# Layer 0 of a two-layer decoder: the context's sixteen key/value products placed at other points of the rounds

## The reference, cut to what matters

```
x = layernorm(x + L0_linear_attention(x))         # 16 heads; q and k normalised per head, scores squared, causal
x = layernorm(x + L0_cross_attention(x, context)) # q, k rms-normed; softmax over the context's 64 tokens
x = layernorm(x + L0_experts(x))                  # 16 experts, top 4, and 2 shared
x = layernorm(x + L1_attention(x))
x = layernorm(x + L1_cross_attention(x, context)) # k = context @ Wk.T, v = context @ Wv.T, 32 heads
x = layernorm(x + L1_experts(x))                  # 8 experts, top 2
```

## Time and profile before

| | us |
|---|---|
| median of 3 runs | 1344.89 |
| lowest, highest | 1341.75, 1347.87 |
| the profiled execution | 1342.68 |
| its span in the profile | 1340.8 |
| TensorE busy in the span | 1170.7 |
| layer 0, up to the first product of the experts' stage | 375.0 |
| mean granted clock of TensorE | 0.932 |

### The profile page before, as it was taken

How to read it: one execution, slowest core, us unless ns; L and a number is a source line. 1 busy time by engine, 2 the same in 40 slices (tenths; PEclk the granted TensorE clock), 3 DMA queues, 4 the chain that set the end, 5 groups by cost and what they waited for, 6 DMA issues and landing times. The chain is left out here.

```text
span 1340.8 us, 29170 instructions
## 1 busy us (share of the span) xinstructions
PE 1170.7 (87%) x10358; PEld 908.3 (68%) x10359; DVE 482.8 (36%) x1215; ACT 531.6 (40%) x1320; POOL 427.2 (32%) x542
## 2 busy tenths in 40 slices
PE   5878988988899759999977888888965999999998
PEld 2576776766546437777755666666653989989997
DVE  1235364554375012323334555544249100000322
ACT  1314435334433213333444566665420434333342
POOL 2022020121036882777624443111104400020343
PEclk9879798899999999999997999998867999999999
DMA  4039619021271434565471110000006665555573
GB/s 148 17 113 363 223 54 334 1 57 59 77 275 70 141 135 121 150 188 149 125 281 66 33 33 17 18 17 2 1 4 211 213 202 162 169 185 185 177 245 103
DMA packets 115225, 171.87 MB, mean 128 GB/s; under 512 B 17424, under 2 KB 92800, under 8 KB 113664
## 3 DMA queue, kind: packets, MB, share of 16 engines
q1 hardware_dynamic: 88640, 127.15, 29.2%
q0 software_dynamic: 9696, 26.75, 6.1%
q10 hardware_dynamic: 16784, 16.49, 3.7%
HBM read 105.07 MB, written 65.27 MB: 127 GB/s over the span
## 5 line engine op out<-in xcount | busy, mean ns | idle before, releaser
L2440 PE MATMUL bank<-m_XGT,m_w 128*128 128x128 f32 x1248 | 150.0, 279 | 1.9 <-issue 1.9
L2440 PEld LDWEIGHTS bank<-m_XGT,m_w 128*128 128x128 f32 x1248 | 146.4, 196 | 3.0 <-issue 2.7
L2454 PE MATMUL bank<-w,m_HT 128*128 x624 | 141.0, 379 | 0.0
L2454 PEld LDWEIGHTS bank<-w,m_HT 128*128 128x128 f32 x624 | 115.7, 190 | 14.1
L2272 ACT ACTIVATE m_HT<-bank,m_b 128x128 f32<-128x128 f32 x312 | 89.1, 369 | 89.7 <-PE bank L2440 77.8
L1478 PE MATMUL bank<-m_W,m_XGT 128*128 x316 | 110.6, 473 | 10.9 <-ACT m_XGT L1337 8.3
L1103 POOL DMA_INDIRECT GA<-ys,r_pos x64 | 64.5, 1008 | 58.3 <-DVE m_US L1419 39.4
L1337 ACT ACTIVATE m_XGT<-bank 128x256 f32<-128x256 f32 x79 | 30.3, 384 | 130.5 <-DVE m_US L1419 84.4
L1478 PEld LDWEIGHTS bank<-m_W,m_XGT 128*128 128x128 f32 x316 | 54.9, 194 | 31.9 <-issue 15.2
L1411 DVE TENSOR_TENSOR m_H<-bank,m_SG 128x176 f32<-128x176 f32 x79 | 27.0, 341 | 136.2 <-ACT m_SG L1341 105.0
L2232 POOL DMA_INDIRECT m_GA<-ys,r_pos x32 | 31.3, 978 | 130.4 <-SPq L2187 121.4
(11 more groups left out here) (356 smaller groups left out, 2441.6 us busy)
## 6 DMA issues: line engine op xcount, KB each, us to landing
m_w<-in_m_w SPq DMA_DIRECT2D x35, 1024.0 KB, 5.3
xs<-zeros SPq DMA_DIRECT2D x1, 10112.0 KB, 34.2
ys<-zeros SPq DMA_DIRECT2D x1, 10112.0 KB, 33.9
ys<-m_US ACTq DMA_DIRECT2D x79, 128.0 KB
m_GS<-xs SPq DMA_DIRECT2D x72, 128.0 KB
w<-in_m_w SPq DMA_DIRECT2D x8, 1024.0 KB, 17.7
m_W<-in_w SPq DMA_DIRECT2D x2, 2816.0 KB, 12.7
xs<-zeros SPq DMA_DIRECT2D x1, 4992.0 KB, 19.8
```

Source lines behind the costliest of these rows:

```text
L2440: last = nc.tensor.matmul(BU[i][:, c * P:(c + 1) * P], w1[:, b, m, lo:lo + P], XGT[:, b % 2, m * P:(m + 1) * P], start=m == 0, stop=m == K ...
L2454: last = nc.tensor.matmul(BY[b % 2][:, 0:DIM], HT[:, b % 2, c, :], w2[:, bass.ds(e, 1), c, :], start=c == 0, stop=c == CH - 1)
```

## The change

Six of the sixteen kv products go to stage 2 of rounds 0, 2 and 4, where `la_var` lies: in each, one in front of the variances and one among them, after the second of the four tiles. In the prologue, whose variances have no kv product, the first `la_v` product of group 0 is placed among them instead. The other ten stand in rounds 6 and 7, in the counts (2, 1, 1, 1) each. Rounds 8 and 9 have none.

A product among the variances and the variances themselves are signalled together (`then_inc(pj.full, 2)`) after the last variance. On ScalarE the product in front is emptied before `exps` of 2 and 3, the one among after the copies of turned weights. The first six tiles are emptied into the last 512 columns of XTA, which the router fills in rounds 8 and 9, and not into `SQK`. Wkv and the first two context tiles are loaded at the start. SyncE's queue follows the order of `fill`: each store, load and zero fill is issued when the use that it depends on comes up in that order.

```diff
-    kv_tiles = iter(range(TILES))
-    for i, counts in ((PAIRS - 2, (1, 1, 1, 1)), (PAIRS - 1, (1, 2, 1, 1)), (PAIRS, (2, 1, 1, 1)), (PAIRS + 1, (2, 0, 0, 0))):
+    kv_tiles = iter(("kv", t, 0) for t in range(TILES))
+    among = {0: ("la_v", 0, 0)}
+    for g in range(1, GROUPS):
+        front, among[g] = next(kv_tiles), next(kv_tiles)
+        fill[2 * (g - 1), 2] = [front] + fill[2 * (g - 1), 2] + [among[g]]
+    KV_EARLY = 2 * (GROUPS - 1)
+    for i, counts in ((PAIRS - 2, (2, 1, 1, 1)), (PAIRS - 1, (2, 1, 1, 1)), (PAIRS, (0, 0, 0, 0))):
         for s, n in enumerate(counts):
-            fill[i, s] += [("kv", next(kv_tiles), 0) for _ in range(n)]
+            fill[i, s] += [next(kv_tiles) for _ in range(n)]
...
+        def kv_staged(t):
+            return (XTA[:, t % 2, TOKENS - GTOK:] if t < KV_EARLY else SQK[:, t % 2, :])
...
+                load_channels(0)
+                load_context(0)
                 sp.dma_start(kvw, io["xb_wkv"].rearrange("(m p) o -> p m o", p=P)).then_inc(fx.ld_kc[0], 16)
                 context(0)
                 context(1)
...
+                for name, g, n in [use for i in range(-1, ROUNDS) for s in range(4) for use in fill[i, s]]:
+                    use = name, g, n
+                    if name == "kv":
+                        pj.wait_emptied(sp, use)
+                        sp.dma_start(fx.kv[g * P:(g + 1) * P, :], kv_staged(g)).then_inc(fx.kv_kept[g % 2], 16)
+                        if g % 2 and g // 2 + 2 < PAIRS:
+                            context(g // 2 + 2)
+                    elif use == ("la_v", g, 1) and g + 1 < GROUPS:
+                        pj.wait_full(sp, use)
+                        load_channels(g + 1)
+                    elif use == ("xa_v", g, 1):
+                        pj.wait_full(sp, use)
+                        if g + 1 < GROUPS:
+                            load_context(g + 1)
+                            if g == 0:
+                                sp.wait_ge(fx.ready, fx.READY)
+                                zero(fx.xs, fx.slots_zeroed, fx.NS0)
+                            elif g == 1:
+                                zero(fx.ys, fx.slots_zeroed, fx.NS0)
+                            else:
+                                zero(fx.xs1, fx.slots_zeroed1, fx.NS1)
+                                zero(fx.ys1, fx.slots_zeroed1, fx.NS1)
+                        else:
+                            shared_weights()
...
-                def inputs(i, s):
+                def inputs(i, s, later=False):
                     for use in fill[i, s]:
                         name, g, m = use
+                        if (use in among.values()) != later:
+                            continue
                         if name == "kv":
                             pj.wait_full(act, use)
                             if g >= 2:
                                 act.wait_ge(fx.kv_kept[g % 2], 16 * (g // 2))
-                            else:
+                            if g == KV_EARLY:
                                 pj.wait_full(act, ("xa_ks", GROUPS - 1, 0))
-                            nc.scalar.activation(SQK[:, g % 2, :], pj.bank(use)[:], ACT.Copy).then_inc(pj.emptied["A"], 1)
+                            nc.scalar.activation(kv_staged(g), pj.bank(use)[:], ACT.Copy).then_inc(pj.emptied["A"], 1)
...
+                    inputs(i, 2, True)
...
+                def keys_and_values(use):
+                    t = use[1]
+                    pe.wait_ge(fx.ld_kc[t // 2 % 2], context_at(t // 2))
+                    return product(nc, pj.bank(use)[:], chunks(KC_T[:, t // 2 % 2], t % 2), [kvw[:, m, :] for m in range(KC)])
+                def values(use):
+                    _, g, n = use
+                    for t in range(2):
+                        last = product(nc, pj.bank(use)[:, t * DIM:(t + 1) * DIM], chunks(XTIN, 2 * n + t),
+                                       [wv[:, m, :] for m in range(KC)])
+                    return last
+                def variance_steps(g, step):
+                    pj.wait_emptied(pe, ("la_k", g, 1))
+                    pj.before_fill(pe, ("la_var", g, 0))
+                    for t in range(TG):
+                        step(t)
+                        last = variances(g, t)
+                        if t == 1:
+                            pj.before_fill(pe, among[g])
+                            (values if g == 0 else keys_and_values)(among[g])
+                    last.then_inc(pj.full, 2)
...
+                    def turn_weights(r):
+                        pe.wait_ge(xw_ready.sem, xw_ready.at(j, r))
+                        for c in range(4):
+                            last = nc.tensor.transpose(SB[r][:, c * P:(c + 1) * P], WX[:, r, c * P:(c + 1) * P],
+                                                       fx.ident[:])
+                        last.then_inc(pt_full.sem, 1)
+                    beside = xa(i) and any(u[0] == "la_var" for u in fill[i, 2])
                     if beside:
-                        pj.before_fill(pe, beside[0])
-                        pj.wait_emptied(pe, ("la_k", beside[0][1], 1))
+                        front, (_, g_next, _), _ = fill[i, 2]
+                        pj.before_fill(pe, front)
+                        keys_and_values(front).then_inc(pj.full, 1)
+                        variance_steps(g_next, turn_weights)
                     else:
                         inputs(i, 2)
-                    if xa(i):
-                        for r in range(RG):
-                            pe.wait_ge(xw_ready.sem, xw_ready.at(j, r))
-                            for c in range(4):
-                                last = nc.tensor.transpose(SB[r][:, c * P:(c + 1) * P], WX[:, r, c * P:(c + 1) * P],
-                                                           fx.ident[:])
-                            last.then_inc(pt_full.sem, 1)
-                            if beside:
-                                last = variances(beside[0][1], r)
-                    if beside:
-                        last.then_inc(pj.full, 1)
+                        if xa(i):
+                            for r in range(RG):
+                                turn_weights(r)
```

More of the change, by code:

```diff
@@ L292, in context, with shared_weights @@
                         "(m p) t -> p m t", p=P)).then_inc(fx.ld_kc[p % 2], 16)
[L294 to L302 removed]
+                def shared_weights():
+                    sp.wait_ge(fx.padded, 1)
+                    for m in range(KC):
+                        for i in range(2):
+                            sp.dma_start(fx.S13[:, m, i, 0:HS].rearrange("p (e h) -> p e h", e=SHARED),
+                                         io["w13"][m, :, E0:EALL, i * I0:(i + 1) * I0]).then_inc(fx.ld_sh, 16)
+                    for c, lo, n, e, at in ((0, 0, P, 0, 0), (1, 0, I0 - P, 0, P), (1, I0 - P, 2 * P - I0, 1, 0),
+                                            (2, 0, HS - 2 * P, 1, 2 * P - I0)):
+                        sp.dma_start(fx.S2[lo:lo + n, c, :], io["w2"][at:at + n, E0 + e, :]).then_inc(fx.ld_sh, 16)
+                load_channels(0)
+                load_context(0)
                 sp.dma_start(kvw, io["xb_wkv"].rearrange("(m p) o -> p m o", p=P)).then_inc(fx.ld_kc[0], 16)
@@ L315, in _ @@
-                for t in range(TILES):
-                    pj.wait_emptied(sp, ("kv", t, 0))
-                    sp.dma_start(fx.kv[t * P:(t + 1) * P, :], SQK[:, t % 2, :]).then_inc(fx.kv_kept[t % 2], 16)
-                    if t % 2 and t // 2 + 2 < PAIRS:
-                        context(t // 2 + 2)
+                for name, g, n in [use for i in range(-1, ROUNDS) for s in range(4) for use in fill[i, s]]:
[22 more added lines that the diff above has]
+                            shared_weights()
@@ L679, in inputs @@
                         name, g, n = use
+                        if use in among.values():
+                            continue
+                        if name == "la_var":
+                            variance_steps(g, lambda t: None)
+                            continue
                         pj.before_fill(pe, use)
@@ L682, in inputs @@
                         if name == "kv":
-                            pe.wait_ge(fx.ld_kc[g // 2 % 2], context_at(g // 2))
-                            last = product(nc, bank[:], chunks(KC_T[:, g // 2 % 2], g % 2), [kvw[:, m, :] for m in range(KC)])
+                            last = keys_and_values(use)
                         elif name in ("la_q", "la_k"):
@@ L690, in inputs @@
                                            [XTIN[:, m, :] for m in range(KC)])
-                        elif name == "la_var":
-                            pj.wait_emptied(pe, ("la_k", g, 1))
-                            for t in range(TG):
-                                last = variances(g, t)
                         elif name == "la_v":
-                            for t in range(2):
```

(3 more changed lines are left out.)

26 lines of the change are left out of this document (2 added, 24 removed).

## The result

The changed kernel is slower, by less than the 0.5% that I gave as the bound, though the interval reaches past it: the ratio of its runs to those of the kernel before is **1.0042, with a 95% interval of [1.0022, 1.0062]**, +5.7 us. Its median is 1353.01 us over 20 runs, that of the kernel before 1346.34 us over 20 runs of its own. The forecast was 1347.8 us with "within 0.5%" as the likeliest, range 1338 to 1355. A second set of runs, in which the kernel before had a median of 1311.5 us, gave 1.0024 [0.9997, 1.0050]. All ratios here leave out runs over 1.5% above the fastest of their kernel and come from kernels run in turns, so they differ from the quotients of the medians, by up to 0.0035.

The account below looks back on a forecast made before the run. Inside layer 0 the rounds wait for TensorE, slowed by half clock around sparse variances and gaps. The terms, 0.5 + 3.3 + 1.0 - 4.1 + 2.2 = +2.9 us, added to 1344.9, gave 1347.8 us; range 1338 to 1355.

Parts of the forecast that it names:

- within 0.5%: Whole kernel: time changes by less than 0.5%, 6.7 us, either way; chance 0.72.
- the likeliest case: Whole kernel: the forecast's own case, +2.9 us to 1347.8 us, own range 1343 to 1352; chance 0.60.
- Prologue: la_v product moved between variance tiles 1 and 2: clock taken to fall, +0.5 us, bounds -3.4 and +1.5.
- Round 0: Front product free in TensorE's 4.23 us gap, second among variances at half clock; +3.3 us together.
- Rounds 2 and 4: Two products each: slots keep full clock, fall comes behind slot 4; +0.5 us each, +1.0 in both.
- the rival in which the clock falls inside the variances: Rounds 2 and 4: second product runs at half, +5.4 us each; total +12.7, 1357.6 us; chance 0.10.
- Rounds 6 and 7: Second product in stage 0 fills the 3.13 us gap, half clock behind it vanishes; -4.1 us, bounds -5.1 and -1.9.
- Rounds 8 and 9: Emptied rounds start the weights' product 3.6 us earlier but lose the clock into the experts; +2.2 us, bounds -3.6 and +4.7.
- SyncE's queue: kv stores behind zero fills hardly blocked, cost 0; rival that they hold up a group's inputs, +8 us, chance 0.05.

Follow-up runs that it names:

- e5_after: The changed kernel run again with no edit, on another chip; ratio to the kernel before 1.0024 [0.9997, 1.0050].
- e2_no_split: The changed kernel with both la_v products of group 0 behind the prologue's variances, as before the change; ratio to the kernel before 1.0005 [0.9965, 1.0046].
- e7_refill: The changed kernel with the prologue as before and three kv products moved from round 7 to rounds 8 and 9; ratio to the kernel before 0.9966 [0.9928, 1.0003].
- e10_best: The changed kernel with prologue and round 0 as before, four early products, two in round 9, dummies in rounds 8 and 9; ratio to the kernel before 0.9958.
- e6_nosplit_dummies: The changed kernel with the prologue as before and dummy products in the gaps of rounds 8 and 9; ratio to the kernel before 0.9918 [0.9883, 0.9953].
- e1_before: The kernel before the change, run and profiled again with no edit; ratio to the kernel before 1.0009 [0.9974, 1.0045].
- e3_dummies: The changed kernel with dummy products written to free banks in the gaps of rounds 8 and 9; ratio to the kernel before 0.9989 [0.9951, 1.0026].
- e11_no_split_again: The changed kernel with the prologue as before, the same program measured a second time on another chip; ratio to the kernel before 0.9951 [0.9922, 0.9981].
- e9_split_only: The changed kernel with all sixteen kv products back in their old places, keeping the prologue's split and loads at the start; ratio to the kernel before 1.0041.

## Why the prediction was right, point by point

**The outcome.** "Within 0.5%" was right, and so was the sign of the likeliest case; the size was +2.9 and measured +5.7 [+3.0, +8.3 by the interval of the ratio]. Most terms held with their mechanism, the prologue was sized too low, and rounds that I had set at nothing took 5.4 us more. So that the whole stayed within 0.5% is in part luck: in the two profiles of the changed kernel layer 0 is 7.8 us longer, not 2.9.

**Prologue: the mis-sized term.** I took +0.5 with bounds -3.4 and +1.5. In the profiles it was +3.5 and -0.8, and +3.1 with the split alone; the first and the last lie beyond my upper bound. The split alone measured 1.0041, which is 5 us [1 to 10], and about 3 us over prologue and round 0 in the profiles. Two things were behind the 3 us. One I had not listed: la_v 1 now follows the variances directly and waits 0.55 us for VectorE to empty them; the la_v product that the change took away from there had covered that. The other I had seen and priced too low. I had read the 6.23 us of the pair as 3.1 us for each product at the half clock, but the clock had risen at 46.0, inside the pair; a product that is at half throughout takes 3.76. And the dense pair behind the variances had ended the half clock after 6.8 us; split by sparse work it did not in three of four profiles with the split, where the half clock lasted 13.7 us (6.8 to 10.2 in those without it). In the fourth, e5_after, the clock held up to the last product, and the prologue was 0.8 shorter than before; my lower bound of -3.4, with the clock full to the end, was never seen.

**Round 0.** +3.3 forecast. The two profiles of the changed kernel show +4.8. Kernels without the split give 48.0 to 50.7 for it and 11.3 to 12.7 for the prologue; together 62.4 in the mean of four against 58.3, +4. The front product lay in the gap, and the other took 3.5 to 3.8 us in all eight profiles that have it, at the half clock as forecast. Not listed was the 0.45 us that xa_v waits for the bank, in all eight.

**Rounds 2 and 4.** +1.0 forecast, +0.8 measured, and in both profiles of the changed kernel by the mechanism that was given: all four slots at full, the fall behind the fourth, the weights' product still near half. Over all profiles it is a tendency and not a rule. In the four without early products the clock fell in the third or fourth slot in all eight rounds. In the nine with them it stayed full through all slots in 15 of 18 rounds, and in three it fell at the product among the variances, as in round 2 of e2_no_split:

```profile
150.91 3.13 PE L58 MATMUL bank<-GA 128*128 128x512 f32 x4
...
153.83 1.06 PE L841 MATMUL bank<-ident,l_WX 128*128 128x128 f32 x4
```

So the rival in which the clock falls inside the variances did occur, in a mild form, 3.4 us of half clock, and it is not what decided the time. In some rounds (round 2 of e7_refill and e10_best, round 4 of e6_nosplit_dummies) the clock did not fall behind the fourth slot either. Rounds 2 and 4 take 75.4 to 84.4 us with the four products and 80.3 to 84.3 without them: on the whole their 7.4 us of work cost nothing, since the clock that they keep gives back as much.

**Rounds 6 and 7.** -4.1 forecast, -4.9 measured, the gap 1.42 and 1.20 us and no half clock behind it. But I had taken the half clock behind the old gap as fixed, and it is not: in e1_before, the same kernel as before, the gap of 3.13 us in round 6 has none behind it and the round takes 29.9 us, as in the changed kernel, while its round 7 has 10.2 us of half clock. So the term is -4.0 against the one profile and -5.9 against the other.

**Rounds 8 and 9.** The parts: softmax 3.4 behind the round's start (3.6 forecast), weights' product 11.7 (12.0 forecast), all at half from the router's transposes on, a little ahead of the turns that I had named, into the experts' stage. Sum with the experts' start +2.2 forecast, +2.2 measured; the parts differ and cancel. Up to the weights' product it was -3.9 (forecast -3.6), from there to the experts' start +5.0 (forecast +4.1: the 0.8 that I had credited to the output product's own density did not come, it took 3.78 at half throughout), and +1.1 in the experts' stage (forecast +1.7). That the clock is the price is shown by e3_dummies, 5.0 us at the same start of the weights' product, and by e11_no_split_again, 3.8 us with the same program. The Trainium skill, page "TensorE: Matmul & The Clock Gate", section "HAM oscillation — how this bites in real kernels", says that a wait between bursts of matmuls lets the clock fall. The trace agrees at this place: the clock fell at 357.0 us, inside the wait of 2.34 us in front of the router's transposes.

**Rounds 3 and 5: what was missing.** I had set untouched rounds at 0. They took 75.5 against 70.1 in both profiles of the changed kernel, by a spell of half clock of 10.2 us in round 3 and one of 3.4 in round 5. My first theory after the result was that the split shifts the program onto them. It is not the only cause: e11_no_split_again has 39.2 and 39.2 without the split. Nor is the split alone enough: e9_split_only has 36.4 and 35.0. But it is not cleared either. All three profiles with the split and early products have a round 3 of 39.2 us; of the six with early products and no split one has it; of the three with neither, none. And the kernels with and without the split lie 9 us apart by their ratios, more than the 3 us of prologue and round 0. That the split or the early products make these spells likelier is possible and not shown. What decides them stays open.

**SyncE's queue.** 0 forecast. In both profiles of the changed kernel TensorE waits for no transfer between 22 us and the experts' stage, so the stores held up no group's inputs.

## What to carry to other kernels

A dense product (one of many columns, that keeps TensorE streaming) is worth its place twice: by the gap that it fills and, often, by the clock that it keeps for the sparse work around it. Before moving one, look at what it had covered where it stood: here a PSUM bank's turn (0.55 us) and the full clock of two whole rounds (4 to 5 us). Where nothing real is left to fill a chain of short waits, dummy products on a free bank can pay: they took such rounds from 30.0 to 25.0 us, and with them and without the split the kernel was 0.8% faster than the one before. And a round's length in one profile is one draw: take the same kernel's profile twice before explaining a difference of 4 us.

## What the runs showed of the hardware

Executions of one program on one chip spread over 12 to 28 us where ten or more were taken (1302 to 1326 us for the kernel before in one set, 1303 to 1319 in another). In the profiles of layer 0 nearly all of the difference is in TensorE's clock: identical matmuls took 1.84 or 3.41 us. Lengths of whole rounds come in steps: round 3 took 35.0 us in eight profiles, 39.2 in four and 36.4 in one. Among the places where the clock fell are waits of 2.3 to 4.2 us (inside them or just behind) and stretches in which TensorE was busy all of the time with matmuls of 4 and 8 columns (13.50 of 13.50 us at half in round 2 of the kernel before).

The sets of runs differ by more than any of these changes: the kernel before has medians of 1346, 1339, 1312 and 1310 us, so a single number from another chip would have shown any of them, of either sign. The clock does not explain this: the middle granted clock of its runs was 0.932, 0.934 and 0.935 in the last three sets. What does was not looked for.
